# Head loop of a fused conv and attention kernel: nine extra TensorE products ahead of the next quad's first scores

## The reference, cut to what matters

```python
q = jnp.concatenate([qn, qr], -1)                    # 16 heads x 64
k1 = jnp.concatenate([kn, broadcast(kr)], -1)
o1 = _attn(q, k1, v1, causal)                        # all earlier tokens
o2 = _attn(q, ks, vs)                                # 256 selected tokens
o3 = _attn(q, kw, vw, winmask)                       # a window of 64 tokens
o = g[:, 0] * o1 + g[:, 1] * o2 + g[:, 2] * o3
return o.transpose(0, 2, 1, 3).reshape(B, T, N_HEAD * VDIM) @ Wproj
```

## Time and profile before

| | us |
|---|---|
| median of 3 runs | 2766.28 |
| lowest and highest | 2761.93 and 2774.25 |
| the profiled execution | 2755.48 |
| its span | 2751.5 |
| TensorE busy | 2476.1 (90% of the span) |
| VectorE busy | 1885.7 (69%) |
| ScalarE busy | 1462.4 (53%) |
| GpSimd busy | 1309.9 (48%) |
| granted TensorE clock, mean over the span | 0.944 |

### The profile page before, as it was taken

How to read it: one execution, slowest core, us unless ns; L and a number is a source line. 1 busy time by engine, 2 the same in 40 slices (tenths; PEclk the granted TensorE clock), 3 DMA queues, 4 the chain that set the end, 5 groups by cost and what they waited for, 6 DMA issues and landing times. The chain is left out here.

```text
span 2751.5 us, 52837 instructions
## 1 busy us (share of the span) xinstructions
PE 2476.1 (90%) x17187; PEld 1731.3 (63%) x17187; DVE 1885.7 (69%) x3715; ACT 1462.4 (53%) x2524; POOL 1309.9 (48%) x884
## 2 busy tenths in 40 slices
PE   5599996765899999999999999999999999999777
PEld 3466664554566666666666666666666666666766
DVE  2767764667486776877767768677686776877526
ACT  1124553332366657666576665666666657666223
POOL 0213681000245637557375573664746647457235
PEclk8699998877999999999999999999999999999788
DMA  3003310011431121120211202122112121120242
GB/s 113 1 12 87 68 26 9 1 46 58 112 87 43 33 51 35 43 55 15 51 35 43 55 15 51 35 47 51 29 38 44 38 51 35 43 55 15 74 139 69
DMA packets 85079, 131.61 MB, mean 48 GB/s; under 512 B 16224, under 2 KB 60769, under 8 KB 84625
## 3 DMA queue, kind: packets, MB, share of 16 engines
q1 hardware_dynamic: 81328, 123.16, 17.7%
q0 software_dynamic: 3024, 7.43, 0.8%
q10 hardware_dynamic: 656, 0.09, 0.0%
HBM read 63.49 MB, written 20.79 MB: 31 GB/s over the span
## 5 line engine op out<-in xcount | busy, mean ns | idle before, releaser
L2467 ACT ACTIVATE a_PT<-PS 128x512 f32<-128x512 f32 (+1 forms) x1111 | 613.7, 586 | 343.0 <-PE PS L2330 235.5
L2188 POOL TENSOR_TENSOR a_KT<-a_PT 128x512 f32<-128x512 f32 (+2 forms) x179 | 418.5, 2353 | 466.0 <-ACT a_PT L2467 464.0
L2188 POOL TENSOR_TENSOR a_KT<-a_KT,a_PT 128x2048 f32<-128x2048 f32 (+3 forms) x128 | 391.8, 3061 | 8.8
L2536 DVE TENSOR_REDUCE a_NM<-PS 128x2 fp32r<-128x512 f32 x460 | 297.1, 687 | 120.2 <-PE PS L2280 116.5
L2329 PE MATMUL PS<-a_QH,a_KSW 128*128 128x256 f32 (+2 forms) x848 | 305.2, 379 | 7.1 <-ACT a_PT L2467 7.1
L2329 PE MATMUL PS<-a_QH,a_K 128*128 128x512 f32 (+3 forms) x768 | 306.9, 406 | 0.0
L2550 DVE TENSOR_REDUCE a_MX<-PS 128x1 f32<-128x512 f32 (+3 forms) x432 | 267.3, 665 | 39.2 <-PE PS L2291 21.2
L2330 PE MATMUL PS<-a_QL,a_K1B 76*128 76x512 f32 (+3 forms) x768 | 262.1, 348 | 0.0
L2291 PE MATMUL PS<-a_K,a_QH 128*128 128x512 f32 (+3 forms) x768 | 253.2, 397 | 0.0
L2277 PE MATMUL PS<-a_KSW,a_QH 128*128 128x512 f32 x460 | 196.2, 476 | 29.4 <-DVE a_QL L2520 29.4
L2523 DVE TENSOR_TENSOR a_KSW<-PS,a_KSW 64x512 fp32r<-64x512 f32 x170 | 117.2, 690 | 126.6 <-ACT a_KSW L2426 123.4
(11 more groups left out here) (437 smaller groups left out, 5573.1 us busy)
## 6 DMA issues: line engine op xcount, KB each, us to landing
a_KWB<-a_KSW SPq DMA_DIRECT2D x68, 256.0 KB, 3.3
a_K1B<-a_K SPq DMA_DIRECT2D x32, 512.0 KB, 5.3
a_XC<-latents SPq DMA_DIRECT2D x17, 512.0 KB, 3.9
a_CKS<-latents SPq DMA_DIRECT2D x17, 512.0 KB, 4.6
a_CF<-latents SPq DMA_DIRECT2D x17, 448.0 KB, 4.1
slots<-in_empty_slots SPq DMA_DIRECT2D x1, 5160.0 KB, 18.7
f_XB<-slots SPq DMA_DIRECT2D x8, 645.0 KB, 8.9
c_EX<-in_experts SPq DMA_DIRECT2D x1, 4608.0 KB, 17.3
```

Of the source, the lines that this page charges most:

```text
L2188: nc.gpsimd.tensor_tensor(total, one_in, other_in, ALU.add).then_inc(s["added"], 1)
L2467: nc.scalar.activation(PT[:, to:to + width], turning(key)[:, 0:width], ACT.Exp).then_inc(s["taken"], 1)
L2536: ins = nc.vector.tensor_reduce(out, bank.rearrange("p (a n) -> p a n", a=2), AX.X, ALU.max, negate=True)
```

## The change

`near_scores` now waits in two steps for `near.0.0`: first for its bank, then it issues nine products of 128 x 384 (bf16) into that bank, then it waits for the splits, and then come the scores, which write the bank from the start. The nine products read the identity and the masks, and nobody reads their result. They are in the loop (once a pass, 16 times) and in the part ahead of it (once). For every other `near` step the same waits stand as before, in two calls. `keep_clock` gets the bank as an argument.

```diff
                 def near_scores(key, q, at):
                     _, i, h = key
                     made = {0: ("s", "w0", "q0"), 2: ("w1", "q1"), 4: ("q2",), 6: ("q3",)}[i] if h == 0 and i % 2 == 0 else ()
-                    after(pe, q, at, bank_free(key, q), *(("reduced", ("split", "tr", g)) for g in made))
                     bank, k0, w = ring(key), max(0, i - 1) * 128, 256 if i else 128
+                    after(pe, q, at, bank_free(key, q))
+                    if i == 0 and h == 0:
+                        keep_clock(9, bank)
+                    after(pe, q, at, *(("reduced", ("split", "tr", g)) for g in made))
                     c, qh = h * SPAN, QH[:, h, i * 128:(i + 1) * 128]
...
-                def keep_clock(count):
+                def keep_clock(count, bank=P[7]):
 
                     for _ in range(count):
-                        nc.tensor.matmul(P[7][:, 0:384], identb[:, :], masks.rearrange("p a n -> p (a n)"), start=True, stop=True)
+                        nc.tensor.matmul(bank[:, 0:384], identb[:, :], masks.rearrange("p a n -> p (a n)"), start=True, stop=True)
```

## The result

| | before | changed |
|---|---|---|
| median | 2764.11 us (4 runs) | 2803.81 us (4 runs) |
| lowest and highest | 2754.14 and 2774.25 | 2793.65 and 2808.72 |
| profiled execution | 2755.48 | 2808.72 |

The change makes the kernel slower: the ratio is 1.0144, 95% interval 1.0115 to 1.0173, or 39.7 us between the medians. The forecast was 2801 us, +35.2.

What follows compares the result with a forecast made beforehand. The prediction took TensorE to bound the kernel, busy for 90% of the span. Products at 25.2 us plus further clock falls at 10.0 us made 35.2 us, on the median of 2766.28 us 2801 us, range 2784 to 2813.

Steps and rivals of the forecast that it cites:

- What bounds the kernel: In the head loop TensorE is busy 109.6 of 112.6 us a pass, so an added product costs its own time.
- Nine products, 17 times, 25.2 us: At near.0.0, in 16 passes and once ahead of the loop: 0.165 us a product, 25.2 us in all.
- Nothing given back: None of the loop's three later TensorE waits, for transposes, an exponential or a maximum, shrinks: 0 us.
- The covered case: Rival: the products' lateness only eats into the 1.64 us wait of near.4.0; 2769 us, chance 0.06.
- The third wait: TensorE's wait for an exponential in the head loop, 7.1 us, was to keep its size.
- The clock, 8 further falls x 1.25 = 10.0 us: Behind near.4.0: low clock in 10 of 15 passes against 2 now, 1.25 us each, 10.0 us more.
- The rule of the Trainium skill: The clock is granted by freely running windows, so falls behind near.4.0 change with the pass's length; sum 35.2 us.
- the two sums: In the head loop: 35.2 us by the rule of freely running windows, 25.2 us by the settled passes alone.
- The products and nothing else: Rival: falls in the loop stay rare because the new pass length also settles; 2791.5 or 2789 us, chance 0.24.
- The gain: Rival: the products at near.0.0 hold the clock, both falls go and the lateness is covered; 2764 us, chance 0.02.

Runs made afterwards that it cites:

- e2: The changed kernel with nine further products in the wait of near.4.0, at the pass's start, into bank 7; 2770.28 us, ratio 1.0041 to the kernel before.
- e1: The kernel before with nine products in the start wait in front of near.4.0, none at near.0.0; 2747.84 us against 2758.24, ratio 0.9966.
- e3: The changed kernel with 21 products at near.0.0 in place of nine; 2812.50 us, ratio 1.0197 to the kernel before.
- e9: The changed kernel with 3 products at near.0.0 in place of nine; 2807.05 us, ratio 1.0205 to the kernel before.
- e7: The changed kernel with the nine products in front of near.0.3 in place of near.0.0; 2794.12 us, ratio 1.0149 to the kernel before.
- e11: The changed kernel itself, unchanged, run and profiled again; 2800.26 us over a before of 2750.99, ratio 1.0177.
- e8: The kernel before with nine products in the start wait, 18 in front of near.2.0 ahead of the loop, and WP loaded first; 2743.02 us, ratio 0.9961.
- e12: The changed kernel with 3 products at near.0.0 in place of nine, and nine in the start wait; 2760.50 us against 2764.19 before, ratio 0.9996.

## Why the prediction was right

**What bounds the kernel.** Right. TensorE sets the pace, and a product put where it is busy costs its spacing. The nine products did not stand in a wait for low parts of queries: the loop has none there, and the two waits end on the same split. Both timelines of the result show it.

**Nine products, 17 times, 25.2 us.** Right. 0.165 us a product was forecast and 0.162 measured (e2 against e1), so 17 x 9 x 0.162 = 24.8 us.

**Nothing given back.** Right for the products. The start wait stayed, 1.78 us for 1.70, and the wait of line 2328 for the last maximum is 12.6 us in both profiles. The covered case (2769 us) is out. The third wait did not keep its size as forecast, 4.0 us for 7.1, but it shrank by the low clock: in e2, with the same nine products and no fall, it is 6.1 us in 15 passes.

**The clock, 8 further falls x 1.25 = 10.0 us.** The mechanism was right: the low clock comes behind the start wait, whether it comes depends on the moment, and a pass of another length meets it at other moments. That was argued before; e3, e9, e7 and the filled kernels show it. The term was sized too small. The prediction took two of three passes and one stretch each, 10 in all. The two profiles of the change have falls in 15 and 14 passes, many double, 21 and 19 stretches. It took 2 for the kernel before, from one profile; the other two have 7, an error the other way. The price of 1.25 us was nearer. By fourteen passes a stretch costs 1.21 us in the first profile of the kernel before, 1.32 in the other two, 1.50 in e7, where all are single, and (1624.70 - 1583.42) / 28 = 1.47 us in e9, where all are double. What moves the price of a single one is when it comes. Against the 114.08 us of e2's passes, the change's second pass (114.89 us, the clock low from the first scores on) lost 0.8 us and its fourteenth and fifteenth (115.57 and 115.67 us, a fall 1.5 to 1.9 us behind the first scores) lost 1.5 and 1.6: the early fall swallows the wait of line 2332. With 12 to 19 stretches more at 1.3 to 1.5 us the term is 16 to 28 us, against 39.7 - 24.8 = 15 us between the medians here and 49.3 - 24.8 = 24.5 us in e11.

So the closeness of 2801 to 2803.81 us is in part luck: the term forecast at 10.0 us was 15 in this comparison and 24.5 in the other, whose +49.3 us lie above the range's high end of +47.

**The rule of the Trainium skill**, "TensorE: Matmul & The Clock Gate", section "What's actually happening", that the clock is granted by windows which run freely and don't start with the kernel: the traces agree. Equal waits of 1.7 us had a fall or had none (e9 and e3), and which of the two followed the length of the pass. Of the two sums that I set against each other, 25.2 and 35.2 us, the rule's was the nearer to 39.7.

**The rivals.** "The products and nothing else" had 0.24 on the ground that a new length may settle at a good moment as well. At 9 products it does not, at 21 it does. What I had not listed is the third outcome, which 3 products have: to settle at a bad one. "Against it: 1.49 us is a large step" was no argument, since the smallest step that was tried cost the most. The gain had 0.02, and rightly: there was neither a wait nor a low clock at this place. Put into the wait that TensorE has, the same nine products did bring 10 us.

**Not foreseen:** the waits of 4.6 to 4.7 us marked "issue", one in the first profile of the change and two in the second, none in any other kernel's head loop. The one in the first profile cost some 2 us, an estimate: the two passes around it took 234.3 us (2032.38 to 2266.68) where a single and a double pass take 232. The trace shows what comes with them. From the second to the fifteenth pass the queue of instructions, q8, otherwise moves nothing in any kernel here, but in each of the three passes with such a wait it moves nine packets of 16 KB, the first of them as the wait begins. So code was loaded again. These are its rows for the wait at 2142.81, for the rest of that pass and for the page of each kernel, 53 packets with one such wait against 44 before; e11 has 62 with two.

```profile
q8 instruction: 3, 0.05, 3.9%
q8 instruction: 6, 0.10, 0.4%
q8 instruction: 53, 0.87, 0.1%
q8 instruction: 44, 0.72, 0.1%
```

Why it was loaded again in these passes alone, and only in this kernel, is open; no run was made for it.

## What to carry to other kernels

Products that nobody reads only pay inside a wait, so check first, on the timeline and by the event that frees their bank, that TensorE waits there; elsewhere they cost their spacing in every pass. A loop with one short wait a pass can hold a low clock or keep free of it for the whole loop, and a change of half a microsecond in the pass's length can switch one into the other, at almost seven times the edit's own cost (56 us for 8 in e9); compare low stretches in the trace before a few per cent are put down to the edit itself, and profile more than once. Filling that wait took the switch away in all kernels that had it filled (e1, e2, e8, e12), and only then could the products be priced.

## What the runs showed of the hardware that I had not expected

- The length of the pass as a function of the added work is not monotone. In fourteen passes 3, 9, 15 and 21 products more gave 1624.7, 1625.8, 1633.8 and 1626.9 us, and with the start wait filled 3 and 9 gave 1583.4 and 1597.2.
- Two kernels whose undisturbed passes differ by 2.9 us, e9 with 3 products and e3 with 21, both ran a dozen and more passes of 116.03 to 116.05 us, the one with a double low stretch in each, the other with none. That the clock's own rhythm holds them there fits all profiles, as in e9 the fall keeps its distance of 1.1 to 1.2 us from the first scores to the end; it was argued from them and not tested by itself.
- Behind a wait of 1.7 us and one of 0.5 us TensorE fell to 1.2 GHz for 6.8 us in every pass of e9. Behind the same two waits (1.73 and 0.48 us) e3 kept 2.4 GHz in the last thirteen passes. What differs is the moment at which they met the clock.
- A single low stretch cost 0.8 us when it began with the first scores and 1.6 us when it came 1.9 us later.
